# One turn of 24 groups in the engines' loop in place of two turns of twelve

## What is computed

```python
h = jnp.maximum(_layernorm(x, axis=-1), 0.0)
x = x + _L0_gnn_ref(h, adj, L0_gnn_Wq, L0_gnn_bq, L0_gnn_Wk, L0_gnn_bk, L0_gnn_Wv, L0_gnn_bv, L0_gnn_beta)
h = jnp.maximum(_layernorm(x, axis=-1), 0.0)
x = x + _L1_gnn_ref(h, adj, L1_gnn_Wq, L1_gnn_Wk, L1_gnn_Wv, L1_gnn_bv, L1_gnn_Wo, L1_gnn_bo)
```

## Time and profile before

| what | us |
|---|---|
| median of three runs | 2221.32 |
| the profiled execution's own time | 2218.76 |
| its span, first to last instruction | 2216.9 |
| TensorE busy | 2158.5 (97%) |
| ScalarE busy | 2049.2 (92%) |
| VectorE busy | 1821.3 (82%) |
| GpSimd busy | 1511.6 (68%) |

### The profile page before, as it was taken

One profiled execution on the slowest core, in us unless ns is written; L12 is line 12 of the kernel. 1 busy time (PEld: TensorE's weight loads), 2 busy tenths in 40 slices (PEclk: granted clock), 3 DMA queues, 4 the chain that ended last, 5 costly groups with the idle time before them and its releaser, 6 DMA issues.

```text
span 2216.9 us, 75650 instructions
## 1 busy us (share of the span) xinstructions
PE 2158.5 (97%) x19968; PEld 1422.1 (64%) x19968; DVE 1821.3 (82%) x10202; ACT 2049.2 (92%) x7824; POOL 1511.6 (68%) x2407
## 2 busy tenths in 40 slices
PE   5999999999999999999999999999999999999997
PEld 2566666666666666666666666666666666666665
DVE  5888888888888888888888888888888888888787
ACT  4999999999999999999999999999999999999987
POOL 1567766767667767667676677676676766776665
PEclk9999999999999999999999999999999999999999
DMA  9886776678678778675795686787767866766752
GB/s 191 168 134 140 130 138 147 130 131 157 126 137 138 137 143 141 132 143 125 134 159 127 136 139 136 145 136 137 143 130 135 154 130 134 146 132 134 133 103 60
DMA packets 461362, 303.38 MB, mean 137 GB/s; under 512 B 228481, under 2 KB 460929, under 8 KB 460929
## 3 DMA queue, kind: packets, MB, share of 16 engines
q1 hardware_dynamic: 460928, 298.45, 71.2%
HBM read 71.83 MB, written 25.17 MB: 44 GB/s over the span
## 4 chain that ended last, share of the span: by engine, by line
PE 84%; DVE 7%; ACT 4%; issue 3%; DMA 1%; SPq 0%; DVEq 0%; POOL 0%; ACTq 0%
PE job_bank L999 46%; PE pt_bank L1022 13%; PE o_bank L1035 8%; PE score_bank L1012 7%; ACT probs L667 3%; PE inv_bank L1058 3%; PE post_bank L1068 2%; PE post_bank L1069 2%; PE post_bank L1072 2%; PE post_bank L1050 2%; DVE neg L787 2%; DVE part_lo L865 1%; DVE inv_wide L857 1%; DMA x_norm<-in_x 1%; DVE off_zero L848 1%
## 5 line engine op out<-in xcount | busy, mean ns | idle before, releaser
L667 ACT ACTIVATE probs<-neg,neg_max 128x128 f32<-128x128 f32 x3072 | 1189.8, 394 | 47.0 <-DVE neg_max L787 47.0
L999 PE MATMUL job_bank<-h,w_hi 128*128 128x512 f16 x2304 | 725.9, 381 | 27.1 <-DMA h<-o_norm 21.6
L667 ACT ACTIVATION_READ_ACCUMULATOR probs<-neg,neg_max 128x1 f32 x3072 | 596.0, 194 | 0.0
L692 ACT ACTIVATE probs_t<-pt_bank 128x512 f32<-128x512 f32 x768 | 450.1, 586 | 32.0 <-PE pt_bank L1022 29.2
L1022 PE MATMUL pt_bank<-ident,probs 128*128 128x128 f32 x3072 | 464.2, 274 | 11.8 <-ACT probs_t L692 11.4
L999 PE MATMUL job_bank<-h,w_lo 128*128 128x512 f16 x1152 | 438.4, 381 | 0.0
L1022 PEld LDWEIGHTS pt_bank<-ident,probs 128*128 128x128 f32 x3072 | 365.9, 141 | 95.9 <-issue 14.0
L599 POOL TENSOR_TENSOR pair_sum<-neg 128x256 f32<-128x256 f32 x384 | 281.0, 732 | 196.0 <-DVE neg_max L787 180.8
L999 PE MATMUL job_bank<-w_hi,h 128*128 128x384 f16 x1536 | 413.9, 326 | 0.6 <-DVE v L879 0.3
L787 DVE CUSTOM_DVE_ANT_0 neg<-score_bank,bias 128x128 f32<-128x128 f32 x1536 | 354.1, 286 | 23.7 <-issue 22.2
L787 DVE CUSTOM_DVE_ANT_0 neg<-score_bank,adj 128x128 f32<-128x128 f32 x1536 | 353.8, 286 | 13.2 <-issue 10.5
(11 more groups left out here) (75 smaller groups left out, 3507.6 us busy)
## 6 DMA issues: line engine op xcount, KB each, us to landing
stack<-part_hi SPq DMA_DIRECT2D x768, 128.0 KB, 3.5
stack<-part_lo SPq DMA_DIRECT2D x384, 128.0 KB, 3.8
x_res<-in_x SPq DMA_DIRECT2D x32, 768.0 KB, 5.8
out_x<-result_rows SPq DMA_DIRECT2D x128, 192.0 KB, 3.4
x_norm<-in_x SPq DMA_DIRECT2D x30, 768.0 KB, 6.2
adj<-in_adj SPq DMA_DIRECT2D x64, 256.0 KB, 3.8
h<-h_rows SPq DMA_TRANSPOSE x252, 3.9
x_norm<-in_x SPq DMA_DIRECT2D x4, 192.0 KB, 4.0
```

The source lines that it names most:

```text
L667: last = act.activation(probs[c % 2][:, h, :], neg[c % 2][:, h, :], ACT.Exp, bias=neg_max[:, b, first + h:first + h + 1], scale=-1.0, accu ...
L692: act.activation(probs_t[b % 2][:, first:first + HC, :].rearrange("p h q -> p (h q)"), pt_bank[:, :], ACT.Copy).then_inc(probs_t_ready, 1)
L999: last = pe.matmul(to, stationary, moving, start=(m == 0), stop=(m == MATMULS - 1))
```

## The change

The loop's step, and with it the number of groups that are written out in its body, goes from 12 to 24. The loop then counts from 3 while i is under 26 + 2 - 24 = 4: once, with i = 3. The compare-and-branch at the end of the body is reached once on each engine and falls through. The body is twice as long.

```diff
--- before.py
+++ after.py
@@ -154,7 +154,7 @@
                 for j, m in self.part(t, r) if m == MATMULS - 1]
 
 
-FIRST_LOOP, LAST_LOOP, TURN = 3, GROUPS - 6, 12
+FIRST_LOOP, LAST_LOOP, TURN = 3, GROUPS - 6, 24
 
 
 def kept(g):
```

## The result

| | before | after |
|---|---|---|
| median of six runs each | 2221.28 | 2210.52 |
| lowest and highest run | 2217.97, 2223.24 | 2209.20, 2212.02 |
| the profiled execution | 2218.76 | 2209.57 |
| its span | 2216.9 | 2207.8 |

The change makes the kernel faster, by more than the 0.2% that the prediction set as its measure: the ratio is 0.9954, with an interval of 0.9943 to 0.9966. In us that is 10.8 between the medians and 9.2 between the profiled executions, where 8.3 were forecast. Three of the six runs of before are the three that the forecast started from.

A forecast was written before the change was run, and what follows sets the result against it. TensorE, busy for 97% of the span, was taken as the bound. Branch 2.8, registers 2.4, turn starts and ends 0.5 and long pairs 2.7 sum to 8.4; the loop's 8.3 was used: 2221.3 - 8.3 = 2213.0 us, range 2211.2 to 2216.8.

The forecast's parts named there:

- The branch, 2.8: End of the loop's first turn: without the taken branch, its pair gets 2.80 us shorter against an ordinary pair.
- the branch and one start of a turn less the long pairs of the second half: Whole loop, a rival: only the branch goes, registers stay; gain 2.2 us, time 2219.1, chance 0.12.
- Registers, 2.4: Loop's 24 pairs: group numbers become constants, so register instructions go; 0.10 us a pair, 2.4 us in all.
- the prediction's sign: TensorE's wait for inv_wide in the loop: 0.23 to 0.25 us each if the forecast is right, 0.29 before.
- Starts and ends of a turn, 0.5: First and last pairs of a turn: 0.4 us for two starts setting up registers, 0.1 for the last pair.
- The long pairs, 2.7: Pairs 2, 3, 7, 8 of each turn: excess from block ends where VectorE is awaited; all 2.7 us goes.
- mostly hidden: Block ends in the loop, a rival's reading: they cause no long pairs, which stay; gain 5.6 us, 2215.7, chance 0.1.
- The third rival: Loop's pairs: block ends recur at sensitive waits (inv_wide, v), up to 2229.8 us; chance 0.03 slower, 0.03 within 0.2%.
- Behind the loop, 0: Last 375 us: same work, code elsewhere in its blocks; 0 taken, bounds 0.4 us gained to 1.5 lost.
- The number of instruction blocks that are fetched hardly moves: Instruction fetch, 265 pieces on queue 14: claimed nearly unchanged, as a turn already fetches all its code again.
- the 0.2 to 0.3 that a run spreads: Whole time: allowance for run variation in the range's lower end, 2211.2 us, beside 0.4 behind the loop.
- the 2.6 us between the median and the profiled execution: Whole time: three runs' median 2221.32 against profiled 2218.76; forecast made on the median, 2213.0, instead of 2210.5.

The follow-up runs named there:

- The kernel with one turn and registers: Kernel before with step 24 but loop end 5 instead of 4, so its variable has two possible values and registers stay; 2216.91 us, ratio 0.9985.
- The announced target: Kernel before with its loop built with hint_back_edge=True; loop 1620.14 us, 2.9 less than before, pair of the taken branch 67.42 us in place of 70.18.
- the near branch: Changed kernel with an empty loop of two turns on every engine between pairs 11 and 12; 2211.60 us, ratio 0.9959 to before.
- the two shifts: Changed kernel with 60, or with 6, one-column memsets at the start of VectorE's stream; 2213.16 us (0.9972 to before) and 2209.34 us (0.9958).
- the shift of 60: Changed kernel with 60 one-column memsets at the start of VectorE's stream; 2213.16 us, ratio 0.9972 to before, loop 1616.87 us.
- the kernel of four turns: Kernel before with step 6 in place of 12, three branches taken, registers kept; 2225.85 us, ratio 1.0027.
- the twelve turns: Kernel before with two groups a turn in place of 12, eleven branches taken, registers kept; 2250.0 us, ratio 1.0140.

## Why the prediction was right, and where it missed

- **The branch, 2.8: right.** The kernel with one turn and registers gains 2.5 in the loop, where the branch and one start of a turn less the long pairs of the second half made 2.2. The announced target removes the stall at the back edge, the near branch has none, and eleven branches cost 3.06 each on average, though single ones lie between 2.5 and 4.6. The rule of the Trainium skill, "Runtime: NRT & Kernel Launch", section Instruction fetch mechanics, that a taken branch to code outside what is held forces a fetch before execution goes on, agrees with these runs. The figure of 108 ns from "Advanced Engine Details and Errata", Control Flow Timing, is near that of the branch that falls through on TensorE's queue (83 ns), and fits neither the near one taken there (377) nor the far one (4546). On the other engines' queues the taken branch of before lasts 74 ns at most and the pause comes behind it.
- **Registers, 2.4: right.** With them ordinary pairs last 67.33 to 67.40, without them 67.27 to 67.28. The wait for inv_wide, 0.24 us in the ordinary case as the prediction's sign had it, is one part of the 0.1 us a pair; TensorE's own busy time, 67.09 against 67.03, is the other.
- **Starts and ends of a turn, 0.5:** half shown. The 0.20 of the second turn's start goes with the branch: that pair lasts 67.58, 68.42 and 68.57 in three executions of before; the first turn's start shows an excess in one of the three (67.53, 67.36, 67.38).
- **The long pairs, 2.7: nearly all, and for the reason given.** Of eight, one and a half remain: 0.35 in pair 2 and 0.13 in pair 4. That a block's end on VectorE makes them is shown by the two shifts and by the places of the pauses, whole multiples of 128 instructions apart. The counts explain the pattern. In the trace of after the four engines other than TensorE have 27,708 instructions, and queue 14 fetched 217 pieces: 128 instructions a piece (queue 8's 162 pieces and TensorE's 41,612 instructions make 257). In the loop of before VectorE has 461 instructions a pair, register instructions included, and five pairs are 2305, one more than 18 pieces: so the places come back every five pairs. In constant code a pair has 385, one more than three pieces: there the ends move by a single instruction from pair to pair, and a place that is hit is hit in neighbouring pairs, as in pairs 7 to 10 with the shift of 60. The Trainium skill's "mostly hidden" for the crossing of a block (same page and section), which the prediction set against this, does not hold where TensorE waits for VectorE: the one wait compared above is 0.35 us longer.
- **The third rival** had this mechanism right (ends that recur at the same place) and its extent wrong: the remainder of one instruction moves a hit on again, after some four pairs.
- **Behind the loop, 0: right.** 0.21 between the profiled executions, and none of it in long pairs.
- **"The number of instruction blocks that are fetched hardly moves": wrong,** with no cost of its own in the sum. Queue 14 fetched 48 of 265 pieces fewer; with one turn and registers it fetched 256, so that 39 of the 48 come from the instructions that are gone.
- **The step that failed** is the term for the spread in "How the numbers follow": "the 0.2 to 0.3 that a run spreads". It came from three runs that lay 0.3 apart. The runs of before span 3.0 to 6.0 us in each of four series (2217.97 to 2224.18 over all), those of after 2.5 and 2.8 in two. The same step carried the 2.6 us between the median and the profiled execution over to the changed kernel; there it measured 0.95 (2210.52 against 2209.57). Against the profiled execution the working gave 2210.5, and 2209.57 came, with 0.86 of the difference ahead of the loop, where first openers lie between 218.1 and 219.0 in the six executions above. So 2210.52 lies 2.5 under the 2213.0 and 0.7 under the range's lower end; with 3 us for the spread, half of the widest series, that end would have stood at 2210.
- **The size of the gain** was not off in the loop: 8.3, forecast and measured. Over the whole time it was under: all 53 runs of before have a median of 2220.6 and all 12 of after 2211.4, a gain of 9.2. The 10.8 of the first series are thus in part chance, and so is part of the miss. The 0.9 between 8.3 and 9.2 lies outside the loop and within what single executions vary; whether the change has a part in it stays open.

## To carry over

Price a change by a stretch that repeats (here the loop, which agrees within 0.8 us between executions), and take the width of the absolute forecast from many runs, since three that agree may do so by chance. Here a loop with a body of two, six or twelve groups paid 2.5 to 4.6 us for every taken branch, on all engines at once, and 0.1 us a pair for the registers that carry its variable; with one turn and a variable of one value both went. An empty body cost nothing; how long a body may be before the stall appears no run shows. Where one engine only just keeps another from waiting, a shift of a few instructions in its stream moves a pair by 0.35 us: compare layouts before reading meaning into half a microsecond.

## What the runs showed of the hardware that was not expected

- A far branch's stall moves rather than goes when its target is announced: 2.76 us less in the pair at the back edge, then 1.98 us of standing on ScalarE at the exit, where the branch falls through (2.30 on VectorE).
- TensorE's part of the stall varies for the same code. Its wait behind the branch was 2.67, 2.52 and 1.71 us in three executions of before, and the branch's pair with the next one lasted 137.76, 138.47 and 137.79: in the third, where the opener waits 0.96 less, the next pair gives it back, and in the second the next pair is 0.85 longer with hardly less of a wait. Openers of the second and of the third execution:

```profile
1031.18 0.39 PE L999 MATMUL job_bank<-h,w_hi 128*128 128x512 f16 x1 [2.52 <-issue]
```

```profile
1030.48 0.39 PE L999 MATMUL job_bank<-h,w_hi 128*128 128x512 f16 x1 [1.71 <-issue]
...
1099.04 0.39 PE L999 MATMUL job_bank<-h,w_hi 128*128 128x512 f16 x1
```

- The stall can draw a second cost behind it. In the kernel of four turns the granted clock stood at full ahead of a stall of 2.8 us at the third turn, and was 0.60 in the three us from 1035, that is at 1.2 GHz for most of them; the same follows the stall of the fourth turn (0.56 in the three us from 1446), and the twelve turns show it behind four of their eleven. There the branch's pair and the next one cost 3.7 to 4.1 us over two ordinary ones, against 2.5 to 2.7 behind the other seven. In the profiled executions of before it didn't happen behind the branch. Windows of the four turns:

```profile
1035.00:1038.00 3.00, 2.79 (x13) 1.84 (x14) 2.23 (x14) 3.00 (x13) 0.92 (x1) 0.60 0.05 15
...
1446.00:1449.00 3.00, 3.00 (x14) 1.70 (x13) 2.76 (x16) 2.92 (x15) 0.35 (x1) 0.56 0.02 5
```
